# Attention: who splits each item's row maxima into a high and a low part, and where they are kept

## The reference, cut to what matters

```
hn = _layernorm(x, ln1_g, ln1_b)
q, k, v = ...                       # 2 batches of 2048 tokens, 16 heads of 16
scores = jnp.einsum('bhqd,bhkd->bhqk', q, k) / jnp.sqrt(jnp.float32(D))
attn = jax.nn.softmax(scores, axis=-1)
o = jnp.einsum('bhqk,bhkd->bhqd', attn, v)
```

## Time and profile before

| | |
|---|---|
| median of three runs | 3111.86 us (3110.77 to 3113.92) |
| profiled execution, its own time | 3100.91 us |
| its span, first to last instruction | 3099.1 us |
| mean granted TensorE clock | 0.958 |
| busy: PE, DVE, ACT, POOL | 2848.4, 2556.4, 1757.2, 990.3 us |
| line 871, reductions to maxima | 1303.7 us in 2560 |
| line 847, exponentials | 991.4 us in 1024 |

### The profile page before, as it was taken

One profiled execution on the slowest core, in us unless ns is written; L12 is line 12 of the kernel. 1 busy time (PEld: TensorE's weight loads), 2 busy tenths in 40 slices (PEclk: granted clock), 3 DMA queues, 4 the chain that ended last, 5 costly groups with the idle time before them and its releaser, 6 DMA issues. The chain is left out here.

```text
span 3099.1 us, 37558 instructions
## 1 busy us (share of the span) xinstructions
PE 2848.4 (92%) x13168; PEld 1460.1 (47%) x13168; DVE 2556.4 (82%) x4154; ACT 1757.2 (57%) x2146; POOL 990.3 (32%) x588
## 2 busy tenths in 40 slices
PE   7988999989989766999999999999999998959998
PEld 5533434434434323444444444444444442648887
DVE  7459999999999986999999999999999993732222
ACT  4457567567666530677777777777777776101110
POOL 3336667666666644010010100101000000434443
PEclk9989999999999885899999999999999999779999
DMA  7523244343343318544565445554455501656663
GB/s 246 202 89 104 88 116 110 97 114 103 95 117 97 93 31 110 68 72 75 65 87 73 74 74 64 87 73 74 74 63 73 73 11 39 112 139 207 197 208 107
DMA packets 199974, 309.95 MB, mean 100 GB/s; under 512 B 97597, under 2 KB 142038, under 8 KB 185324
## 3 DMA queue, kind: packets, MB, share of 16 engines
q1 hardware_dynamic: 182380, 259.96, 40.0%
q0 software_dynamic: 17408, 47.65, 6.4%
HBM read 237.08 MB, written 53.36 MB: 94 GB/s over the span
## 5 line engine op out<-in xcount | busy, mean ns | idle before, releaser
L871 DVE TENSOR_REDUCE attn_mx<-attn_pX 128x1 f32<-128x512 f32 (+1 forms) x2560 | 1303.7, 575 | 69.8 <-PE attn_pX L776 27.9
L847 ACT ACTIVATE attn_pr<-attn_pS 128x1024 f32<-128x1024 f32 x1024 | 991.4, 1021 | 443.2 <-PE attn_pS L788 443.2
L776 PE MATMUL attn_pX<-attn_ks,attn_qs 48*128 48x512 f32 (+1 forms) x2560 | 897.6, 438 | 46.3 <-DMA attn_vs<-v_d 25.1
L776 PEld LDWEIGHTS attn_pX<-attn_ks,attn_qs 48*128 48x128 f32 x2560 | 446.0, 188 | 664.4 <-DVE attn_mx L871 560.4
L1489 DVE TENSOR_TENSOR_SCAN mamba_h<-mamba_pA,mamba_hs,mamba_db 128x512 f32<-128x512 f32 x512 | 616.1, 1262 | 19.1 <-ACT mamba_pA L1211 19.1
L788 PE MATMUL attn_pS<-attn_qs,attn_ks 50*128 50x512 f32 x2048 | 626.2, 436 | 3.4 <-ACT attn_pr L847 3.4
L1355 PE MATMUL mamba_pY<-mamba_g,mamba_ident 128*128 128x512 f32 x1024 | 497.0, 630 | 113.1 <-DVE mamba_g L1502 113.1
L1108 POOL TENSOR_TENSOR mamba_db<-mamba_bq,mamba_u 128x2048 f32<-128x2048 f32 x128 | 580.7, 4537 | 11.6 <-DVE mamba_u L1448 11.6
L798 PE MATMUL attn_pO<-attn_pr,attn_vs 128*17 128x512 f32 x4096 | 539.8, 599 | 0.7 <-ACT attn_pr L847 0.7
L1211 ACT ACTIVATE mamba_pA<-mamba_dt,held_an 128x512 f32<-128x512 f32 x512 | 352.2, 690 | 299.5 <-DVE mamba_h L1489 296.1
L1355 PEld LDWEIGHTS mamba_pY<-mamba_g,mamba_ident 128*128 128x128 f32 x1024 | 193.5, 198 | 406.7 <-DVE mamba_g L1502 205.4
(11 more groups left out here) (231 smaller groups left out, 1992.5 us busy)
## 6 DMA issues: line engine op xcount, KB each, us to landing
mamba_bq<-bc_d SPq DMA_DIRECT2D x64, 1024.0 KB, 5.3
attn_ks<-parts_d SPq DMA_DIRECT2D x192, 256.0 KB, 9.2
exp_w<-in_w SPq DMA_DIRECT2D x46, 1024.0 KB, 5.7
attn_vs<-v_d SPq DMA_DIRECT2D x32, 544.0 KB, 15.9
parts_d<-proj_qp SPq DMA_DIRECT2D x32, 512.0 KB, 5.6
attn_qs<-parts_d SPq DMA_DIRECT2D x192, 64.0 KB, 8.4
oraw_d<-attn_oe SPq DMA_DIRECT2D x32, 256.0 KB, 2.1
mamba_dt<-held_e POOLq DMA_DIRECT2D x14, 512.0 KB, 7.6
```

Of the source, the lines that this page charges most:

```text
L776: pe.matmul(pX[bank(s, e)][:, 0:width], QS[slot][rows, pair, qt * P:(qt + 1) * P], KS[slot][rows, pair, keys:keys + width], start=True, st ...
L847: act.activation(PR[2 * (kt % 2) + pair][:, :, :], pS[pair][:, :, :], ACT.Exp, scale=HD ** -0.5).then_inc(p_sb, 1)
L871: dve.tensor_reduce(MX[:, col, a:a + 1], pX[bank(s, e)][:, 0:width], AX.X, ALU.max).then_inc(x_max, 1)
```

## The change

The copy and the subtraction are issued by GpSimd. VectorE keeps the reduction to `MN` (now `largest`) and the transpose, and goes on with the first five reductions of the next item between them. For that `MX` has two buffers, chosen by the item's parity. A semaphore `m_found` counts both VectorE's reduction to `MN` and GpSimd's copy, and `m_split` counts the subtraction. GpSimd's work for the row chunks becomes a function `rows_in`, called after the split of item 3c+2. The start of the phase has one more fill of `MX`.

```
-        MX = m.sb("mx", [P, NSM, 2])
+        MX = [m.sb(f"mx{n}", [P, NSM, 2]) for n in range(2)]
...
+                def split(n):
+
+                    pool.wait_ge(m_found, 2 * n + 1)
+                    if n >= 1:
+                        pool.wait_ge(m_turned, n)
+                    pool.tensor_copy(MS[:, 0, :], MN[:, :]).then_inc(m_found, 1)
+                    pool.wait_ge(m_found, 2 * n + 2)
+                    pool.tensor_tensor(MS[:, 1, :], MN[:, :], MS[:, 0, :].bitcast(F32), ALU.subtract
+                                       ).then_inc(m_split, 1)
...
+                split(0)
+                for n in range(NI - 1):
+                    split(n + 1)
+                    if n % 3 == 1 and n // 3 < NCH:
+                        rows_in(n // 3)
...
+                        if n == 0 and i * RING + s >= 2:
+                            dve.wait_ge(m_found, 2 * (i * RING + s) - 3)
...
-                def split(i, s):
+                def largest(i, s):
 
-                    chain.at(i * (RING * 2) + (s * 2 + 1))
                     dve.wait_ge(x_max, i * (RING * NRED) + (s + 1) * NRED)
-                    chain.step(dve.tensor_reduce(MN[:, :], MX[:, :, :].rearrange("p (x a) b -> p x (a b)", a=QC),
-                                                 AX.X, ALU.max, negate=True))
-                    chain.step(dve.tensor_copy(MS[:, 0, :], MN[:, :]))
-                    dve.tensor_tensor(MS[:, 1, :], MN[:, :], MS[:, 0, :].bitcast(F32), ALU.subtract
-                                      ).then_inc(m_split, 1)
+                    if i * RING + s >= 1:
+                        dve.wait_ge(m_split, i * RING + s)
+                    dve.tensor_reduce(MN[:, :], MX[s % 2][:, :, :].rearrange("p (x a) b -> p x (a b)", a=QC),
+                                      AX.X, ALU.max, negate=True).then_inc(m_found, 1)
...
                 def body(i, s, left):
                     if left >= 1:
                         maxima(i, s + 1, LEAD, NSM)
-                        split(i, s + 1)
+                        largest(i, s + 1)
+                    if left >= 2:
+                        maxima(i, s + 2, 0, SM_KT)
+                    if left >= 1:
                         turned(i, s + 1)
                     if left >= 2:
-                        maxima(i, s + 2, 0, LEAD)
+                        maxima(i, s + 2, SM_KT, LEAD)
```

More of the change, by code:

```diff
@@ L613, in phase_attention @@
         x_max = m.sem("x_max")
-        mchain_s = m.sem("mchain")
+        m_found = m.sem("m_found")
         m_split = m.sem("m_split")
@@ L697, in _ @@
                 max_rows(0, 0)
-                sp.wait_ge(filled, 2)
+                sp.wait_ge(filled, 4)
                 sp.dma_start(ids_d.rearrange("(p n) o -> p (n o)", p=P), FILLI[:, :]).then_inc(ids_out, 16)
@@ L744, in _, with rows_in @@
                 pool.wait_ge(w_in, 16 * 6)
-                for c in range(NCH):
+                def split(n):
[6 more added lines that the diff above has]
+                                       ).then_inc(m_split, 1)
+                def rows_in(c):
                     pool.wait_ge(pv_done, (3 * c + 2) * KT)
@@ L855, in _ @@
             def _(dve):
-                chain = Chain(dve, mchain_s)
+                chain = Chain(dve, filled)
                 dve.memset(pO[:, :], 0.0).then_inc(o_sb, 1)
-                chain.step(dve.memset(MX[:, :, :], -3.0e38))
-                dve.memset(FILL[:, :], float(nobody)).then_inc(filled, 1)
-                dve.wait_ge(filled, 1)
+                for n in range(2):
+                    chain.step(dve.memset(MX[n][:, :, :], -3.0e38))
+                chain.step(dve.memset(FILL[:, :], float(nobody)))
                 dve.tensor_copy(FILLI[:, :], FILL[:, :]).then_inc(filled, 1)
@@ L870, in maxima @@
                             dve.wait_ge(x_ps, i * (RING * NRED) + (s * NRED + e + 1))
-                            dve.tensor_reduce(MX[:, col, a:a + 1], pX[bank(s, e)][:, 0:width], AX.X, ALU.max
+                            dve.tensor_reduce(MX[s % 2][:, col, a:a + 1], pX[bank(s, e)][:, 0:width], AX.X, ALU.max
                                               ).then_inc(x_max, 1)
-                def split(i, s):
-                    chain.at(i * (RING * 2) + (s * 2 + 1))
+                def largest(i, s):
                     dve.wait_ge(x_max, i * (RING * NRED) + (s + 1) * NRED)
-                    chain.step(dve.tensor_reduce(MN[:, :], MX[:, :, :].rearrange("p (x a) b -> p x (a b)", a=QC),
-                                                 AX.X, ALU.max, negate=True))
-                    chain.step(dve.tensor_copy(MS[:, 0, :], MN[:, :]))
-                    dve.tensor_tensor(MS[:, 1, :], MN[:, :], MS[:, 0, :].bitcast(F32), ALU.subtract
-                                      ).then_inc(m_split, 1)
+                    if i * RING + s >= 1:
+                        dve.wait_ge(m_split, i * RING + s)
+                    dve.tensor_reduce(MN[:, :], MX[s % 2][:, :, :].rearrange("p (x a) b -> p x (a b)", a=QC),
+                                      AX.X, ALU.max, negate=True).then_inc(m_found, 1)
                 def turned(i, s):
@@ L890, in _ @@
                 maxima(0, 0, 0, NSM)
-                split(0, 0)
+                largest(0, 0)
+                maxima(0, 1, 0, SM_KT)
                 turned(0, 0)
-                maxima(0, 1, 0, LEAD)
+                maxima(0, 1, SM_KT, LEAD)
                 def body(i, s, left):
```

## The result

| | before | changed | changed, second time |
|---|---|---|---|
| median | 3112.89 us (4 runs; 3112.68 in 9 beside the second time) | 3090.24 us (4 runs) | 3094.6 us (5 runs) |
| ratio to before | | 0.9924 [0.9908, 0.9939] | 0.9938 [0.9925, 0.9952] |
| profiled execution | 3100.91 us | 3084.59 us | 3094.9 us |
| its span | 3099.1 us | 3082.5 us | 3092.8 us |

The change makes the kernel 24 us faster by the first ratio (19 to 29), 19 us by the second (15 to 23). The forecast was 3093.4 us, 18.5 us less.

What follows compares the result with a forecast made beforehand. TensorE and VectorE were taken to set the pace together. 30 splits at 0.60 us (18.0 us) plus 0.5 for item 0, other terms 0, gave 18.5 us off 3111.86: forecast 3093.4 us, range 3087 to 3101.

Steps and rivals of the forecast that it cites:

- What bounds the phase: Steady attention stretch: TensorE and VectorE set the pace together; a VectorE delay costs only beyond 0.16 us of slack per step.
- What the change removes: VectorE at the split: 0.88 us from line 898 to the next reduction becomes 0.21, giving back 0.67 us.
- The rival by which an instruction holds the queue to its end: VectorE's split: line 898 holds 0.32 us, the transpose 0.21; 11 to 16 us saved, 3098 us, chance 0.2.
- How much reaches the step: The split's step: costs 0.24 us over an ordinary one instead of 0.84, saving 0.60 us per item.
- The transpose: VectorE's queue: standing five reductions later it takes 0.14 us, covered by TensorE's own delay, cost 0.
- GpSimd: Copy and subtraction there: ready 0.98 us behind line 898's end, 1.4 us before the transpose's place, cost 0.
- The slower rival: Transpose waiting for GpSimd: at the upper bound each item loses 1.8 us, +54 us, 3166 us; chance 0.04.
- SyncE: DMAs of the maxima: issued 1.95 us later, the last still 5.5 us ahead of the next item's scores, cost 0.
- The sum: Whole kernel: 18.5 us saved, profiled execution 3082.4 us, timed runs 3093.4 us.
- The term for the steady stretch: Attention's steady stretch: 30 splits at 0.60 us each save 18.0 us.
- The 0.5 us for item 0: Opening at half clock: VectorE gets 0.67 us back at the first split, less 0.14 for the transpose.
- the load of about 6 us that the prediction weighed: GpSimd's first call of a freshly loaded routine: would cost 4 us once, saving 14.5 us instead of 18.5.

Runs made afterwards that it cites:

- placed: bank_after with the reduction to 16 maxima two blocks later, where VectorE stands idle, and the transpose five reductions behind it: 3086.81 us, ratio 0.9914.
- vector_spread: Changed kernel with copy and subtraction back on VectorE, five reductions behind each of the first three instructions, maxima 32 blocks ahead instead of 24: 3099.63 us, ratio 0.9962.
- bank_before: Kernel before the change, with the three PSUM banks of maxima taken in turn across group borders: 3113.11 against 3114.95 us, ratio 0.9996.
- bank_after: Changed kernel with the three PSUM banks of maxima taken in turn across the borders of four-item groups: 3091.35 us, ratio 0.9934.
- late_short: Changed kernel with one 128x1024 fill (about 1 us) on GpSimd ahead of each copy: 3093.34 us, ratio 0.9932.
- placed_lead5: placed with the maxima 20 blocks ahead instead of 24: 3132.9 us, ratio 1.0058.
- late_long: Changed kernel with four 128x1024 fills on GpSimd ahead of each copy, each waiting for the one before: 3232.71 us, ratio 1.0372.
- pool_alone: Changed kernel with the transpose straight behind the reduction to 16 maxima, no reductions between, copy and subtraction still on GpSimd: 3120.74 us, ratio 1.0017.

## Why the prediction was right, and where it was off

**What bounds the phase.** Right. The slack of 0.16 us a step is real: a 0.20 us instruction placed in it costs about 0.03 us (`placed`), 0.08 or 0.12 us ones nothing (`vector_spread`). That VectorE is 97% busy and yet takes more work for free is the point that its busy share would have hidden.

**What the change removes.** 0.21 us from line 898 to the next reduction was forecast, 0.20 came. The rival by which an instruction holds the queue to its end is wrong here: 0.286 long, next start at 0.20. The section of the Trainium skill that the prediction names beside it (VectorE: DVE Perf Modes, The DRAIN you can't avoid) also says that a next op that is not held starts earlier, which the prediction left out. The trace agrees with that part, for instructions that don't read what the one ahead writes.

**How much reaches the step.** 2.87 us forecast for the split's step, 2.81 measured, and a distance of 42.4 against 42.39. For 23 of 30 items the working holds to 0.06 us.

**What was missing.** I took one split for all of them. At seven of 30 the step before the split's is 3.23, the split's own step is an ordinary one, and the item gains 0.20 in place of 0.62: the bank numbering skips one at a group's border. 30 x 0.60 = 18 us became 23 x 0.62 + 7 x 0.20 = 15.7 us. The trace of before has the sign of it, step pairs of 3.24 and 2.86 at every fourth split; I read one split and took it for all. `bank_before` and `bank_after` show that the same skip costs 0 in one kernel and 3 us in the other.

**The transpose.** Covered, as forecast; its place was forecast 2.69 us behind line 898's start and measured at 2.68.

**GpSimd.** 0.98 us from the reduction's end was forecast, and the last item, where VectorE waits, shows 0.60: the hops are shorter (0.07 to 0.12 us from VectorE's end to the copy's start in 31 of 32 splits, where I took 0.19). The margin is 1.8 us, not 1.4; `late_short` used up 1.0 of it at no cost. The slower rival's mechanism is real, and its price too low: I priced 30 stalls at their length, and 54 us, and had left out the half clock that comes with them.

**SyncE.** Nothing waited for the maxima's DMAs, as forecast. `placed_lead5` shows that the room I read from the queue (5.5 us behind the last issue) is not all usable: there TensorE wanted the rows 1.4 us behind the end of the last issue, which was enough in 22 items and up to 2.9 us too little in eight.

**The sum.** 18.5 us forecast, 16.3 between the two profiled executions, 19 and 24 by the ratios. The term for the steady stretch was 2.3 us too high (18.0 against 15.7). The 0.5 us for item 0 can't be read from the traces: the first scores come 0.5 us sooner behind the phase's first matmul (61.4 to 60.9), but item 1's maxima are combined 0.6 us later (93.3 to 93.9). The granted clock rose to 1.00 at 68.5 us before and at 70.7 after, and in `bank_before`, whose steady stretch is that of before, at 77.5, with 96.4 in place of 93.3. So the forecast of 3093.4 us lies so near the two medians, 3090.2 and 3094.6, in part by luck: the missed borders took 2.3 us off the gain, and what the timed runs have beyond the trace, 3 to 8 us, put as much or more back. These few us stay unexplained.

## What to carry to other kernels

Where two engines drive each other in turn, read the slack of one ordinary round from start-to-start distances, and place small work into it, one piece a round, with the piece's consumer a round later; who executes it matters less than what waits behind it. When a long stall goes, look for a smaller irregularity that it had covered, a buffer numbering that restarts for one: group the steps of before by length and explain each group. And price a new stall of TensorE with the clock that follows it.

## What the runs showed of the hardware

- **A stall of TensorE costs more than its length.** The granted clock is 1.00 throughout the long stretches of before and after. In `late_long` VectorE waits about 2.1 us and with it a matmul 1.3 to 1.8 us, once an item; in 24 of 30 items a stretch at 0.50, the 1.2 GHz level, of 3.4 to 14 us followed: 62 us of direct waits became 139. In `placed_lead5` it came with all eight waits of 2.5 to 2.9 us. In `pool_alone`, where a matmul's longest wait for VectorE was 0.6 us, it happened twice in 30 items; before the change (0.4 us) and after it (0.2 us) never.
- **Small instructions.** At 128x16 a copy on VectorE holds its queue for 0.08 us when the next instruction is independent, and for 0.21 us when it is not; GpSimd takes 0.20 us for the copy and 0.22 for the subtraction, starts 0.07 or 0.12 us behind VectorE's end, and follows itself 0.08 us behind the end. GpSimd's first copy of the whole kernel started 0.15 us behind VectorE's end and took 0.20 us, with its follower 0.08 us behind it; the load of about 6 us that the prediction weighed did not show.
- **Small DMAs.** Eight transfers of 2 KB, issued within 4.3 us, were in time in 22 items of `placed_lead5` and 2.5 to 2.9 us late in eight, those in which 1 MB of GpSimd's loads ran beside them.
